# Two-layer graph network on one core: the second edge sort ends inside layer 0's batches, with eight pairs per batch weighed five to three

## The chip, the cores and the metric

One core of a Trainium2 chip runs the kernel. The metric is the device time of one execution in microseconds, and the time of the kernel before is the median of three such runs. The profile is of one more execution.

## The reference, cut to what matters

6250 nodes of 512 features, 100,000 edges (src, dst). Layer 0 is a graph attention with 8 heads of 64: for each head, the attention of an edge is a softmax over the edges of its source node, and the weighted features of the destinations are summed per source. Layer 1 sums features over the edges by destination, convolves them, and adds an attention of the first 256 nodes.

```python
feat = x @ W[h]
logit = leaky_relu(alpha_s[src] + alpha_d[dst], 0.2)
e = exp(logit - segment_max(logit, src)[src])
att = e / segment_sum(e, src)[src]
agg = segment_sum(att[:, None] * feat[dst], src)
...
agg = segment_sum(xn[edge_index[0]], edge_index[1]) / max(deg, 1)
conv_out = relu(agg @ W_conv + b_conv)
```

Layer 0 therefore needs the edges sorted by source (sort A), layer 1 the edges sorted by destination (sort B).

## The kernel before, in words

**The front.** Both sorts are bitonic over 2^17 keys, laid out as 128 rows of 1024. VectorE does a stage as two instructions, a minimum (line 2263) and a maximum (line 2264) of 128x512 each (`stage`). The merges from 2^11 to 2^17 each need the rows turned twice: a crossing is eight transposes on TensorE (line 2431, into `psA` for A, into `psCD` for B), a copy of one half by ScalarE (line 2095), and then as many stages as the merge has. Crossing n of a sort (n = 0 to 13) is followed by n/2+1 stages when n is even and by 10 when n is odd; after an odd one comes a change of sign, done by ScalarE for A and by VectorE (line 2272) for B. `ORDER` is the sequence A0 B0 A1 B1 ... A13 B13, which all three engines follow. Between crossings TensorE and ScalarE make layer 0's features, one tile of 128 nodes at a time (`dense`, `turn_h`, `project`, 49 tiles), and `DENSE_AT` says how many tiles go ahead of which crossing of A. B13, the last crossing, with its ten stages, is done on VectorE after the tables of sort A have been made (lines 2334 to 2408), and `slot_fields_of_destinations` (lines 2369 to 2374) then makes `minorB` and `sorted_nodes`.

**Layer 0.** The sorted edges are taken in 55 batches of 16 chunks of 128 edges. GpSimd gathers a batch as 16 indirect DMAs of 128 feature rows (line 517) into a ring of two batches; a slot is free when the lot (a pair of chunks, eight to a batch) that used it two batches earlier has been summed (`lot_ps`). For each batch a chain gives the weights: ScalarE copies the destinations' part of the rows when they have arrived (line 580), TensorE adds, ScalarE copies the logits (line 582), VectorE finds the maxima (`local_runs`, `carry_runs`, `find_tops`, lines 622 to 678), ScalarE takes the exponential (line 560), TensorE turns the weights (line 795). Then the pairs of chunks are weighed: pairs 0 to 5 by VectorE (line 694), 6 and 7 by ScalarE (`weigh_late`, line 568, 16 activations of 128x65 a pair); TensorE multiplies each by a one-hot matrix (`lot`, line 812), and VectorE adds the lot to its tile (`add_lot`, line 704). `OWN = LB - 2` is the number of VectorE's pairs.

What sets the order is `pass_batch(this, nxt)`, written out per engine: while lot a of this batch is done, a step of the next batch's chain is put behind it (on VectorE local_runs at a = 4, find_tops at a = 5, its first two weighings at a = 7). VectorE, ScalarE and TensorE run it as a loop over two batches.

```python
OWN = LB - 2
for a in range(OWN, LB - 1):
    weigh_late(this, a)
...
if 2 <= a + 2 < OWN:
    weigh(this, a + 2)
```

**Layer 1.** Its first steps on VectorE (`layer1_vector`) take the first node of chunks from `sorted_nodes`, then scale and normalise the tiles (line 1333, `x1_slots`), while TensorE does the attention of 256 nodes; then GpSimd gathers again (line 1141).

## Time and profile before

| | us |
|---|---|
| median of three runs (2983.2 to 2986.25) | 2983.75 |
| the profiled execution's own time | 2989.12 |
| its span | 2987.2 |
| TensorE busy in the span | 2509.0 (84%) |
| VectorE busy | 2172.7 (73%) |
| GpSimd busy | 1835.8 (61%) |
| ScalarE busy | 993.7 (33%) |

The span runs from the first to the last instruction of the profiled execution. Its stages, by the timelines: the front to about 411, layer 0's batches to about 1560, layer 1's attention and tables to about 1700, its gathers to about 2700, the convolution and the output to the end. Busy shares are means over all of them, so a stage has to be looked at by itself.

### The profile page before, as it was taken

Reading aid. Unit: us, or ns where it says so; the run is one execution under the profiler, and the core shown is the slowest. Engines: PE = TensorE matmul, PEld = TensorE weight load, DVE = VectorE, ACT = ScalarE, POOL = GpSimd, SP = SyncE. Lnnn points to the kernel's source line nnn. Section 1 sums busy time; section 2 is a strip of 40 time slices with the busy share of each in tenths; the row PEclk is TensorE's granted clock in tenths of the full one; section 3 lists DMA queues with packets and bytes.
Section 4 is the critical chain, followed back from the end, with each engine's and each line's share of the span. In section 5 each row is a group of like instructions: output and inputs, shape, how many; then the busy total and the mean of one; then the engine's idle time right before and its main releaser. Section 6 shows DMA issues by size and latency. Waiting matters only on the chain. (4 is left out here: it accounts for less than half of the span.)

```text
span 2987.2 us, 46040 instructions
## 1 busy us (share of the span) xinstructions
PE 2509.0 (84%) x10691; PEld 1549.3 (52%) x10692; DVE 2172.7 (73%) x3788; ACT 993.7 (33%) x3078; POOL 1835.8 (61%) x1881
## 2 busy tenths in 40 slices
PE   5887728999999999999988888888888889999990
PEld 4555416777777777777766733333333333334440
DVE  8999988898888888888988655434444444445668
ACT  6843335555555555555553600000000000002220
POOL 0000036777777777777748267777777777774658
PEclk8998858999999999999997999999999999999995
DMA  6110047888888888888757877777777777774217
GB/s 208 52 40 37 37 136 217 240 243 246 243 239 245 245 239 245 244 244 240 245 189 227 269 247 210 210 210 209 210 210 210 210 210 210 210 209 124 67 56 295
DMA packets 243450, 588.26 MB, mean 197 GB/s; under 512 B 57744, under 2 KB 82832, under 8 KB 243400
## 3 DMA queue, kind: packets, MB, share of 16 engines
q0 software_dynamic: 133120, 443.52, 50.6%
q1 hardware_dynamic: 110280, 144.14, 14.7%
q8 instruction: 23, 0.38, 0.0%
q14 instruction: 27, 0.22, 0.0%
HBM read 533.43 MB, written 54.10 MB: 197 GB/s over the span
## 5 line engine op out<-in xcount | busy, mean ns | idle before, releaser
L517 POOL DMA_INDIRECT big<-feat_table,idx x880 | 839.0, 953 | 688.1 <-ACT idx L542 408.1
L1141 POOL DMA_INDIRECT big<-h_table,idx x784 | 741.4, 946 | 303.3 <-issue 216.2
L812 PE MATMUL psA<-big,onehot 128*128 128x260 f32 x1760 | 440.3, 393 | 16.1 <-DVE big L694 13.9
L812 PE MATMUL psB<-big,onehot 128*128 128x260 f32 x1760 | 433.7, 390 | 7.3
L568 ACT ACTIVATE big<-big,late_weights 128x65 f32<-128x65 f32 x1760 | 434.1, 340 | 0.0
L812 PEld LDWEIGHTS psA<-big,onehot 128*128 128x128 f32 x1760 | 318.3, 191 | 100.4 <-issue 37.0
L812 PEld LDWEIGHTS psB<-big,onehot 128*128 128x128 f32 x1760 | 317.7, 190 | 63.8 <-DVE acc L704 17.6
L542 ACT CAST idx<-minorB 128x8 int32 (+1 forms) x101 | 20.2, 203 | 944.0 <-DMA big<-h_table,idx 944.0
L1570 DVE TENSOR_TENSOR acc<-acc,psCD 128x512 f32 x176 | 120.6, 685 | 205.1 <-PE psCD L1879 203.1
L1570 DVE TENSOR_TENSOR acc<-acc,psA 128x512 f32 x176 | 120.6, 685 | 202.6 <-PE psA L1879 199.9
L1878 PE MATMUL psCD<-big,onehot 128*128 x352 | 185.1, 607 | 45.4 <-ACTq L1294 39.3
L1878 PE MATMUL psA<-big,onehot 128*128 x352 | 184.8, 607 | 42.7 <-ACTq L1294 37.4
L694 DVE TENSOR_TENSOR big<-big,psCD 128x1040 f32<-128x1040 f32 x168 | 204.1, 1229 | 0.0
L694 DVE TENSOR_TENSOR big<-big,psE 128x1040 f32<-128x1040 f32 x162 | 196.8, 1228 | 0.0
L2464 PE MATMUL psB<-big 128*128 128x512 f32 x392 | 184.8, 616 | 0.0
L1905 PE MATMUL psA<-big 128*128 128x512 f32 x392 | 180.8, 605 | 0.0
L1879 PE MATMUL psCD<-big,onehot 128*128 x352 | 179.8, 593 | 0.0
L1879 PE MATMUL psA<-big,onehot 128*128 x352 | 179.8, 593 | 0.0
L704 DVE TENSOR_TENSOR acc<-acc,psA 128x520 f32 x220 | 152.8, 694 | 26.4 <-DVE acc L704 12.6
L704 DVE TENSOR_TENSOR acc<-acc,psB 128x520 f32 x220 | 152.1, 691 | 7.6 <-PE psB L812 3.3
L552 ACT CAST onehot<-psCD 128x1024 f32<-128x1024 bf16 x110 | 111.7, 1015 | 128.2 <-PE psB L812 128.2
L1570 DVE TENSOR_TENSOR acc<-acc,psE 128x512 f32 x88 | 60.3, 685 | 111.5 <-PE psE L1879 110.6
(446 smaller groups left out, 3841.8 us busy)
## 6 DMA issues: line engine op xcount, KB each, us to landing
nodes_all<-slot_nodes SPq DMA_DIRECT2D x56, 512.0 KB
big<-feat_table,idx POOLq DMA_INDIRECT x880, 3.8
feat_table<-big SPq DMA_DIRECT2D x49, 264.0 KB, 2.1
x_table<-acc SPq DMA_DIRECT2D x49, 256.0 KB, 5.8
h_table<-big SPq DMA_DIRECT2D x49, 256.0 KB, 3.7
big<-h_table,idx POOLq DMA_INDIRECT x784, 3.7
big<-h_table SPq DMA_DIRECT2D x49, 256.0 KB, 2.6
big<-x_table SPq DMA_DIRECT2D x49, 256.0 KB, 4.2
```

Source lines behind the costliest of these rows:

```text
L517: g.indirect_dma_start(ring[:, b.k, q * SB + u, :], None, feat_table, bass.IndirectOffsetOnAxis(ap=idx[:, 2 * b.k + q, u:u + 1], axis=0)). ...
L552: s.copy(onehot[:, q, :, :].rearrange("p b n -> p (b n)"), onehot_ps).then_inc(onehot_ready, 1)
L568: ins = s.activation(part, part, ACT.Copy, scale=late_weights[:, at:at + 1])
L694: v.tensor_tensor(pair, pair, weight_ps[b.k][:, 2 * a * H:(2 * a + 2) * H] .rearrange("p (b h) -> p b h", h=H).unsqueeze(3).broadcast_to([ ...
L704: v.tensor_tensor(d, d, (psA, psB)[a % 2][:, :].rearrange("p (u w) -> p u w", u=2)[:, :, 0:HALF_W], ALU.add).then_inc(lot_added, 1)
L812: ins = pet.matmul(psum[:, 512 * hf:512 * hf + HALF_W], onehot[:, q, u % SB, :], ring[:, b.k, u, HALF_W * hf:HALF_W * (hf + 1)], start=(u ...
L1141: g.indirect_dma_start(big[:, place:place + D], None, h1_table, bass.IndirectOffsetOnAxis(ap=idx[:, r.c % CHUNK_CYCLE, b:b + 1], axis=0)). ...
L1570: v.tensor_tensor(d, d, lot1_sums(r, b), ALU.add).then_inc(lot1_added, 1)
L1878: pet.matmul(lot1_sums(r, b), onehot[:, r.q, 2 * b, :], pair[:, 0:D], start=True, stop=False)
L1879: pet.matmul(lot1_sums(r, b), onehot[:, r.q, 2 * b + 1, :], pair[:, D:2 * D], start=False, stop=True).then_inc(lot1_ps, 1)
L1905: ins = pet.matmul(psA[:, q * 512:(q + 1) * 512], aggT[:, q, k * P:(k + 1) * P], Wc_s[:, k, :], start=(k == 0), stop=(k == KD - 1))
L2464: pet.matmul(psB[:, q * D:(q + 1) * D], hTbuf[:, q, k * P:(k + 1) * P], W4[:, k, :, :].rearrange("p h o -> p (h o)"), start=(k == 0), stop ...
```

## The change

Sort B's crossings 8 to 13 (the merges to 2^15, 2^16 and 2^17) leave the front. Their 48 stages (5+10+6+10+7+10) are spread over layer 0's batches by `LatePlan`: 36 batches get one stage and 6 get two (batches 2, 7, 18, 24, 35 and 42, `doubles` = 1), always behind `add_lot` of a = 3. Each of the six crossings is done in two halves in two batches of their own (four transposes on TensorE after lot 6, one copy of 128x512 on ScalarE after the feed); in 9 of those 12 batches VectorE has no stage. ScalarE does the two late changes of sign. VectorE weighs pairs 0 to 4, ScalarE 5, 6 and 7. The remaining crossings of B are cut into parts between A's (`B_PARTS`), and `DENSE_AT` has new numbers. The loops over batches on VectorE, ScalarE and TensorE are written out (SyncE and GpSimd keep theirs). `minorB` and `sorted_nodes` are made in layer 1's first steps. The late stages use `tables` and a new `late_keys`, in whose space `minorB` and `nodeB` lie; the tile table and the pads share `pad_space`.

```diff
+        FRONT_BITS = 14
+        FRONT_B = 2 * (FRONT_BITS - ROW_BITS)
+        B_PARTS = {0: [(0, 0, 17)], 1: [(1, 0, 5)], 2: [(1, 5, 17)], 3: [(2, 0, 17)], 4: [(3, 0, 5)], 5: [(3, 5, 17)], 6: [(4, 0, 17)], 7: [(5, 0, 5)], 8: [(5, 5, 17)], 9: [(6, 0, 17)], 10: [(7, 0, 4)], 11: [(7, 4, 7)], 12: [(7, 7, 17)]}
+        ORDER = [(kind, n) for na in range(CROSSINGS)
+                 for kind, n in [("A", na)] + [("B", nb) for nb, first, _ in B_PARTS.get(na, ()) if first == 0]]
+        assert [n for kind, n in ORDER if kind == "B"] == list(range(FRONT_B))
+        DENSE_AT = {("A", n): count for n, count in enumerate((17, 0, 4, 1, 4, 1, 3, 1, 3, 2, 3, 2, 3, 2))}
...
+                at, batch, turned = self.first_at, 0, FRONT_B
+                self.stages, self.crossings, self.copied, self.flips = {}, {}, {}, {}
+                for n in range(FRONT_B, CROSSINGS):
+                    m = ROW_BITS + 1 + n // 2
+                    needed = step
+                    for half in range(2):
+                        turned, step = turned + 1, step + 1
+                        self.crossings[batch + half] = (half, needed, at, turned)
+                        self.copied[batch + half] = step
+                    at, batch = at ^ 1, batch + 2
+                    js = list(range(ROW_BITS - 1, -1, -1) if n % 2 else range(m - ROW_BITS - 1, -1, -1))
+                    first = batch
+                    while js:
+                        count = 2 if batch - first < doubles else 1
+                        for j in js[:count]:
+                            self.stages.setdefault(batch, []).append((j, step, at))
+                            at, step = at ^ 1, step + 2
+                        js, batch = js[count:], batch + 1
+                    batch -= 1
+                    if n % 2 and m < ALL_BITS:
+                        self.flips[batch] = (m + 1, step, at)
+                        at, step, batch = at ^ 1, step + 1, batch + 1
+                self.last_step = step
+                assert at == 0 and batch < BATCHES, (at, batch)
...
-        OWN = LB - 2
+        OWN = LB - 3
...
-                                pool.wait_ge(sortB_done, 2)
+                                pool.wait_ge(look_ready, 1)
...
+            def late_copies(t):
+                if t in late.flips:
+                    m, step, at = late.flips[t]
+                    act.wait_ge(sortB.step, step)
+                    s.activation(late_bufs[at ^ 1], late_bufs[at], ACT.Identity,
+                                 scale=signs[:, m - ROW_BITS:m - ROW_BITS + 1]).then_inc(sortB.step, 1)
+                if t in late.crossings:
+                    half, _, at, turned = late.crossings[t]
+                    act.wait_ge(sortB.turned, turned)
+                    s.copy(late_bufs[at ^ 1][:, half * 512:(half + 1) * 512], (psD, psE[:, :])[t % 2]).then_inc(sortB.step, 1)
...
-            with act.Fori(0, BATCHES // 2) as i:
-                for c in range(2):
-                    feed(Batch(i, c + 1), Batch(i, c))
+            for n in range(BATCHES - 1):
+                feed(batch(n + 1), batch(n))
+                late_copies(n)
...
+            def late_stage(j, step, at):
+                dve.wait_ge(sortB.step, step)
+                a, b = (late_bufs[at].rearrange("p (n two h) -> p n two h", two=2, h=1 << j)[:, :, u, :] for u in range(2))
+                low, high = (late_bufs[at ^ 1].rearrange("p (n two h) -> p n two h", two=2, h=1 << j)[:, :, u, :]
+                             for u in range(2))
+                v.tensor_tensor(low, a, b, ALU.min).then_inc(sortB.step, 1)
+                v.tensor_tensor(high, a, b, ALU.max).then_inc(sortB.step, 1)
...
                             tiles = load_tiles(dve, tileA, this(2, 1))
+                            for j, step, at in late.stages.get(this.c, ()):
+                                late_stage(j, step, at)
...
-            with dve.Fori(0, BATCHES // 2) as i:
-                for c in range(2):
-                    pass_batch(Batch(i, c), Batch(i, c + 1))
+            for n in range(BATCHES - 1):
+                pass_batch(batch(n), batch(n + 1))
             pass_batch(batch(BATCHES - 1), None)
...
+                    if a == LB - 2 and this:
+                        cross_late(this.c)
+                    if a == 4 and this and this.c - 1 in late.copied:
+                        pe.wait_ge(sortB.step, late.copied[this.c - 1])
...
+            def cross_late(t):
+                if t in late.crossings:
+                    half, needed, at, _ = late.crossings[t]
+                    pe.wait_ge(sortB.step, needed)
+                    for b in range(4):
+                        block = (4 * half + b) * P
+                        ins = pet.transpose((psD, psE[:, :])[t % 2][:, b * P:(b + 1) * P], late_bufs[at][:, block:block + P], ident)
+                    ins.then_inc(sortB.turned, 1)
...
-            turn_fields(sortB, 2)
             pass_batch(None, batch(0))
-            pe.wait_ge(sortB_done, 2)
-            with pe.Fori(0, BATCHES // 2) as i:
-                for c in range(2):
-                    pass_batch(Batch(i, c), Batch(i, c + 1))
+            for n in range(BATCHES - 1):
+                pass_batch(batch(n), batch(n + 1))
...
+            act.wait_ge(fields, 2)
             PA.done(s.copy(node_rows, sorted_nodes), "nodes")
+            PA.wait(act, "nodes")
...
-            dve.wait_ge(sortB_done, 2)
+            dve.wait_ge(sortB.step, late.last_step)
+            v.tensor_scalar(sorted_nodes, late_bufs[0].bitcast(I32), SHIFT, MINOR_MASK, ALU.logical_shift_right,
+                            ALU.bitwise_and).then_inc(fields, 1)
+            dve.wait_ge(fields, 2)
...
+            x1_upto(3)
+            low, wrap = keys_flat[:, 0:COLS].bitcast(I32), late_bufs[0].bitcast(I32)
+            dve.wait_ge(fieldsT, 3)
+            link(v.tensor_scalar(low, psC[:, :].bitcast(I32), MINOR_MASK, None, ALU.bitwise_and))
+            link(v.tensor_scalar(wrap, low, float(PAD_MINOR), -float(PAD_MINOR), ALU.is_ge, ALU.mult))
+            v.tensor_tensor(minorB[:, :, :].rearrange("p b r -> p (b r)"), low, wrap, ALU.add).then_inc(sortB_done, 1)
...
+            pe.wait_ge(sortB.step, late.last_step)
+            pe.wait_ge(parts_kept, BATCHES + 1)
+            for b in range(SB):
+                ins = pet.transpose(psC[:, b * P:(b + 1) * P], late_bufs[0][:, b * P:(b + 1) * P], ident)
+            ins.then_inc(fieldsT, 1)
...
+            pe.wait_ge(sortB_done, 1)
...
+                for i, j in list(enumerate(js))[first:end]:
+                    stage(srt, j, False, srt.ps if i == 0 else srt.bufs[:, srt.at, :], srt.bufs[:, srt.at ^ 1, :], True)
+                if n % 2 and m < ALL_BITS and end >= len(js):
+                    if srt is sortB and n == FRONT_B - 1:
+                        dve.wait_ge(srt.step, srt.steps)
+                        v.tensor_scalar(late_bufs[late.first_at], srt.bufs[:, srt.at, :],
+                                        signs[:, m + 1 - ROW_BITS:m + 2 - ROW_BITS], None, ALU.mult).then_inc(srt.step, 1)
+                        srt.steps += 1
+                    else:
+                        flip(srt, m + 1)
```

And in the program of the front:

```diff
-            for kind, n in ORDER[:-1]:
-                if (kind, n) == ("A", 1):
+            for na in range(CROSSINGS):
+                if na == 1:
                     group_rstd0(2)
-                sort_crossed({"A": sortA, "B": sortB}[kind], n)
+                sort_crossed(sortA, na)
+                for nb, first, end in B_PARTS.get(na, ()):
+                    sort_crossed(sortB, nb, first, end)
...
-            sort_crossed(sortB, CROSSINGS - 1)
-            kB, other = sorted_keys_of(sortB)
             dve.wait_ge(rows_loaded, 16)
             for q in range(2):
                 v.tensor_scalar(onehotT[q], nodes_all[:, q, :], iota_col[:, 0:1], None, ALU.is_equal).then_inc(onehotT_ready, 1)
-            slot_fields_of_destinations(kB, other, minorB)
```

How the order moves, at three places. VectorE, the middle of a batch (around `add_lot` of a = 2 and 3; 694/743 is a weighing, 704/753 an `add_lot`, 632/681 the first step of local_runs). Before:

```order
L703 REGISTER_ALU
L704 ISA
L704 TENSOR_TENSOR acc<-acc,psA 128x520
L694 TENSOR_TENSOR big<-big,psCD 128x2x520
L700 REGISTER_ALU
L703 REGISTER_ALU
L704 ISA
L704 TENSOR_TENSOR acc<-acc,psB 128x520
L131 ISA
L131 TENSOR_LOAD tables
L631 REGISTER_ALU
L632 SCALAR_TENSOR_TENSOR alphas<-alphas 128x128
```

Now, in a batch with one stage:

```order
L743 TENSOR_TENSOR big<-big,psE 128x2x520
L753 ISA
L753 TENSOR_TENSOR acc<-acc,psA 128x520
L753 ISA
L753 TENSOR_TENSOR acc<-acc,psB 128x520
L135 TENSOR_LOAD pad_space
L761 TENSOR_TENSOR tables<-late_keys 128x128x4
L762 TENSOR_TENSOR tables<-late_keys 128x128x4
L681 SCALAR_TENSOR_TENSOR alphas<-alphas 128x128
```

The weighing that stood between the two `add_lot` is gone, and a minimum and a maximum between `tables` and `late_keys` stand ahead of local_runs.

ScalarE, from the one-hot copy that ends one feed to the next batch's copy of the destinations' part (580/620). Before:

```order
L552 CAST onehot<-psCD 128x1024
L568 ACTIVATE big<-big,late_weights 128x65 x16
L577 REGISTER_ALU
L580 COPY look_space<-big 128x128
L581 REGISTER_ALU
L582 COPY alphas<-psCD 128x128
L551 REGISTER_ALU
L552 CAST onehot<-psCD 128x1024
```

Now, in a batch that holds half a crossing:

```order
L592 CAST onehot<-psCD 128x1024
L643 COPY late_keys<-psCD 128x512
L608 ACTIVATE big<-big,late_weights 128x65 x32
L620 COPY look_space<-big 128x128
L622 COPY alphas<-psCD 128x128
L592 CAST onehot<-psCD 128x1024
L582 CAST idx<-minorA 128x8 x2
L608 ACTIVATE big<-big,late_weights 128x65 x16
```

32 activations instead of 16 stand ahead of that copy, and in twelve batches the copy of half a crossing as well.

TensorE in the front, from crossing A2 on (2431/2515 is a crossing, `psA` for A and `psCD` for B; 2452, 2464 and 2469 or 2536, 2548 and 2553 are one tile). Before:

```order
L2431 MATMUL psA<-ident_wide,big 128x128 x8
L2431 MATMUL psCD<-ident_wide,big 128x128 x8
L2431 MATMUL psA<-ident_wide,big 128x128 x8
L2431 MATMUL psCD<-ident_wide,big 128x128 x8
L2452 MATMUL psCD<-ident_wide,big 128x128 x4
L2464 MATMUL psB<-big 128x512 x4
L2469 MATMUL psE<-Wa,big 128x16 x4
```

Now:

```order
L2515 MATMUL psA<-ident_wide,big 128x128 x8
L2536 MATMUL psCD<-ident_wide,big 128x128 x4
L2548 MATMUL psB<-big 128x512 x4
L2553 MATMUL psE<-Wa,big 128x16 x4
L2515 MATMUL psA<-ident_wide,big 128x128 x8
L2515 MATMUL psCD<-ident_wide,big 128x128 x8
L2536 MATMUL psCD<-ident_wide,big 128x128 x4
L2548 MATMUL psB<-big 128x512 x4
L2553 MATMUL psE<-Wa,big 128x16 x4
```

A tile stands between A2 and A3, and B2 has moved behind A3, with the next four tiles (the first is shown) behind it.

## Rows read from the trace of the kernel before

**Rows 1.** Work by engine in stretches: busy (instructions) per engine, granted clock, DMA share, GB/s
```profile
150.00:225.00 75.00, 66.07 (x300) 43.18 (x300) 70.77 (x113) 30.40 (x67) 0.00 (x0) 0.93 0.11 40
225.00:300.00 75.00, 60.46 (x264) 38.66 (x264) 73.26 (x116) 26.94 (x60) 0.00 (x0) 0.86 0.10 37
900.00:1100.00 200.00, 182.18 (x1078) 141.97 (x1076) 178.24 (x360) 112.10 (x410) 151.45 (x160) 1.00 0.82 244
```

**Rows 2.** Timeline of GpSimd: start, duration, engine, line, operation, [idle before <- releaser]
```profile
411.44 1.13 POOL L517 DMA_INDIRECT big<-feat_table,idx  x1 [407.49 <-ACT idx L542]
...
466.24 0.94 POOL L517 DMA_INDIRECT big<-feat_table,idx  x1 [4.55 <-PE psA L812]
...
1530.04 0.94 POOL L517 DMA_INDIRECT big<-feat_table,idx  x1 [0.30 <-issue]
...
1700.77 1.05 POOL L1141 DMA_INDIRECT big<-h_table,idx  x1 [49.98 <-DMA h_table<-big]
```

**Rows 3.** Timeline of VectorE in the sort
```profile
157.40 0.69 DVE L2263 TENSOR_TENSOR big<-big,psA 128x512 f32<-128x512 f32 x1
...
223.03 0.69 DVE L2263 TENSOR_TENSOR big<-big 128x512 f32<-128x512 f32 x1
...
224.36 0.69 DVE L2263 TENSOR_TENSOR big<-big 128x512 f32<-128x512 f32 x1
...
252.02 0.75 DVE L2272 TENSOR_SCALAR big<-big,signs 128x1024 f32<-128x1024 f32 x1
...
404.75 0.69 DVE L2334 TENSOR_SCALAR big<-big 128x1024 int32<-128x1024 int32 x1
```

**Rows 4.** Timeline of TensorE in the same stretch
```profile
240.76 0.64 PE L2452 MATMUL psCD<-ident_wide,big 128*128 128x128 f32 x4
...
245.47 1.07 PE L2431 MATMUL psA<-ident_wide,big 128*128 128x128 f32 x8
252.83 1.97 PE L2431 MATMUL psCD<-ident_wide,big 128*128 128x128 f32 x8 [6.28 <-DVE big L2272]
...
261.15 1.07 PE L2431 MATMUL psA<-ident_wide,big 128*128 128x128 f32 x8
```

**Rows 5.** Timeline of VectorE between the sort and the first batch
```profile
445.65 0.49 DVE L2416 TENSOR_SCALAR onehotT<-nodes_all,iota_col 128x1024 bf16<-128x1024 bf16 x1 [8.75 <-DMA nodes_all<-slot_nodes]
...
446.45 0.69 DVE L2369 TENSOR_SCALAR big<-big 128x1024 int32<-128x1024 int32 x1
...
453.52 0.28 DVE L632 SCALAR_TENSOR_TENSOR alphas<-alphas 128x128 f32<-128x128 f32 x1
```

**Rows 6.** Groups of instructions of GpSimd in 417.7:424.2, 425.2:436.3 and 1000:1400
```profile
L517 POOL DMA_INDIRECT big<-feat_table,idx x6 | 5.7, 946 | 1.8 <-issue 1.8
...
L517 POOL DMA_INDIRECT big<-feat_table,idx x9 | 9.3, 1033 | 2.7 <-issue 2.7
...
L517 POOL DMA_INDIRECT big<-feat_table,idx x320 | 304.2, 951 | 97.5 <-issue 87.7 <-PE psB L812 4.9 <-PE psA L812 4.9
```

**Rows 7.** Timeline of ScalarE in one batch
```profile
1003.67 3.95 ACT L568 ACTIVATE big<-big,late_weights 128x65 f32<-128x65 f32 x16
1011.74 0.30 ACT L580 COPY look_space<-big 128x128 f32<-128x128 f32 x1 [4.13 <-DMA big<-feat_table,idx]
...
1022.45 1.01 ACT L552 CAST onehot<-psCD 128x1024 f32<-128x1024 bf16 x1 [2.33 <-PE psB L812]
```

**Rows 8.** Timeline of VectorE in the same batch
```profile
1001.52 2.38 DVE L694 TENSOR_TENSOR big<-big,psE 128x1040 f32<-128x1040 f32 x2
...
1012.92 0.33 DVE L632 SCALAR_TENSOR_TENSOR alphas<-alphas 128x128 f32<-128x128 f32 x1
...
1021.28 2.38 DVE L694 TENSOR_TENSOR big<-big,psCD 128x1040 f32<-128x1040 f32 x2
```

**Rows 9.** Timeline of TensorE, lot 5 of that batch and layer 1's first transposes
```profile
1014.92 1.97 PE L812 MATMUL psB<-big,onehot 128*128 128x260 f32 x8
...
1576.08 1.97 PE L1740 MATMUL psCD<-ident_wide,look_space 128*128 128x128 f32 x8 [8.07 <-ACT look_space L1184]
```

83 lines of the change are left out of this document (37 added, 46 removed).

## The prediction

> **What bounds the kernel now.** I first read the work by engine in stretches, since a share over the span mixes stages. In the front VectorE is busy 94 to 98% [rows 1], TensorE 81 to 88%: the sorts on VectorE set the pace, with TensorE close behind, and TensorE's granted clock falls from 0.93 to 0.86 where it waits more. In layer 0's batches every engine looks full. What bounds them is on GpSimd's timeline: the first gather goes out at 411.44, the first one that had to wait for a lot at 466.24, the last of the 880 at 1530.04 [rows 2]. From 466.24 on that is 847 steps in 1063.8 us, 1.256 us each, and the group of 320 gathers in 1000:1400 has 0.951 busy and 0.30 between two, mostly "issue" [rows 6]: GpSimd never stops. A batch is 16 gathers, 20.1 us. The other engines wait for rows: ScalarE stood idle 4.13 us for a DMA ahead of line 580 [rows 7]. So a microsecond saved on VectorE inside a batch is worth nothing, and one that is added costs nothing while the loop stays under 20.1.
>
> How near is it? VectorE's own loop, from one late_weights copy's first weighing to the next, is 1001.52 to 1021.28, 19.76 us, with hardly a gap ahead of 1012.92 [rows 8]: some 19.65 if it never waited for rows, 0.45 under GpSimd. And there is a cushion: batch 2's first gather is the one at 466.24, so the gather that reuses lot 5's slot of batch 27 (442 steps later) goes out at 1021.4, while that lot ends at 1016.9 [rows 2, 9]. The engines can be 4.5 us late before GpSimd stops.
>
> **The front.** A stage costs 224.36 - 223.03 = 1.33 us, a change of sign 0.75 [rows 3]. Crossings B8 to B12 have 5+10+6+10+7 = 38 stages ahead of sort A's tables, which begin at 404.75: 50.5 us, and two changes of sign, 1.5: 52.0 us off VectorE's path. B13's ten stages (another 13 us) give nothing: they ran while VectorE would otherwise have waited for the nodes, and it still waited 8.75 us after them [rows 5].
>
> Not all of the 52 comes. TensorE's tiles stay (4.71 us each, 240.76 to 245.47), and after an idle of 6.28 us a crossing and a tile took 8.32 us where 1.07 + 4.71 = 5.78 is normal, 2.5 more [rows 4]; this goes with the lower granted clock of that stretch [rows 1]. In the new order TensorE waits at B2 until B1's last five stages are done, and only then has B2 and four tiles ahead of A4: 1.07 + 18.8 + 2.5 + 1.07 + 0.8 for ScalarE's copy (an estimate: half the elements of the 1.01 us copy in rows 7, and two waits) = 24.3 us, while VectorE has A3's ten stages and B2's two, 15.9. Stall: 8.4 us. The same count gives 21.8 - 19.9 = 1.9 at A2 (four tiles behind B1, against 15 stages), about 1.0 at A7 and 2.7 at A10 (three tiles and ScalarE's change of sign against 14 stages); at the others VectorE has more to do than TensorE. Sum 14.0, so the tables start **38.0 us earlier**. Bounds for the stalls: 0 (the front now has next to none, rows 1) and 28, twice my count, because a late tile moves all that follow.
>
> **Up to the first lot.** The nodes' DMA chain hangs on the tables of sort A and moves with them. Behind it `slot_fields_of_destinations` goes away, from 446.45 to 453.52, 7.07 us [rows 5]. Part of it covered the look-up, copies and logits of batch 0, which TensorE and ScalarE did beside it and which VectorE must now wait for. Between 0 and 7.1 I take the middle, **3.4 us**. GpSimd then starts batch 2 some 41.4 us earlier than 466.24, though it waits some 11 us in front of it: 32 gathers at 1.256 take 40 us, and the lot it needs comes 51 us after the first gather.
>
> **Layer 0.** VectorE per batch: one weighing less, 2.38 - 1.23 = 1.15 us [rows 8], and in 36 batches one stage more, 1.33 and about 0.1 for its wait: 19.93, under 20.1. In six batches there are two stages, 21.3, and each makes the loop 1.2 us late, which the cushion of 4.5 takes, and the 13 batches without a stage (18.5) give it back. ScalarE per batch: a pair more, 3.95 us, ahead of line 580, where it stood idle 4.13 [rows 7]: it now arrives 0.2 us before the rows. From 1011.74 to its next one-hot copy at 1022.45 is 10.7, and copy and two pairs are 8.8 more: 19.5. In twelve batches a copy of half a crossing and in two a change of sign come on top, each at most about the 1.01 us of that one-hot copy [rows 7]: 20.5, again within the cushion. Lot 5 now waits for ScalarE: its pair is done about 3.95 us behind 1003.67, so at 1007.6, and the lot starts at 1014.92 [rows 7, 9]. TensorE's 48 late transposes are a half-dozen crossings, 1.07 each. The written-out loops I cost at nothing; they issue one program row after another as the front does, and the cover is the same cushion.
>
> So GpSimd stays the bound, and what counts is what slows a gather. In 425.2:436.3, while VectorE ran B13's stages, nine gathers had a mean of 1.033 us; in 417.7:424.2, six had 0.946 [rows 6]. That is 0.087 us per gather of 1.33 us, so per stage, and 48 stages make **4.2 us**. By the Trainium skill, page "SBUF — State Buffer", section "SBUF: two separate sides", VectorE and GpSimd share a pair of ports as an exclusive lock, which an operation with two SBUF inputs also takes against a GpSimd operation that reads SBUF, and the loser blocks for the whole instruction. The stages have two SBUF inputs, the weighings one; by that rule 96 instructions could each hold a gather for up to their 0.69 us, 66 us in all. The trace shows a sixteenth of it.
>
> **Layer 1.** Inserted ahead of its first tiles are the field of the nodes (0.69 us, as line 2369) and, behind tile 2, three operations of the same kind as lines 2372 to 2374; TensorE's first transposes, at 1576.08 [rows 9], wait for these. VectorE's part is between 0, were it all beside waits, and the 7.07 us that the same four operations and their turn took in a row [rows 5]; the turn is now done before VectorE comes to it, which leaves less than half, and the first transposes follow VectorE closely, so I take **3.0 us**, and it stays to the end because the gathers from 1700.77 [rows 2] are again GpSimd's.
>
> **Sum:** -38.0 - 3.4 + 4.2 + 3.0 = -34.2 us. Against the profiled execution's 2989.12 that is 2954.9; the median of the runs is 5.4 lower, so 2983.75 - 34.2 = **2949.5 us**.
>
> **The rivals.**
> 1. TensorE takes over the front. For it: it is busy 81 to 88% there already [rows 1], and the clock falls with every wait. Against: at most crossings VectorE's stages outlast the tiles. If the stalls are 28 instead of 14, the time is 2963.5.
> 2. VectorE's loop becomes layer 0's bound. For it: only 0.2 us lie between 19.93 and 20.1, and each stage stands straight ahead of the chain that makes the weights. Against: the loop now has gaps of its own that the counts keep. If the weighing's 1.15 us don't come back, because VectorE only waits for lots instead, a batch with a stage takes 21.08: 0.9 times 36, and 2.2 times 6, less the cushion of 4.5, is 41 us, and the time 2983.75 - 34.2 + 41 - 4.2 (GpSimd's slowing no longer counts) = 2986. A third of it (0.3 us a batch) gives about 2959.
> 3. The lock is held. For it: the same two engines, and gathers of 1.033 against 0.946 us [rows 6]. Against: the size. If each late stage stops GpSimd for its 1.38 us, 48 of them are 66 us, the sum -34.2 - 4.2 + 66 = +27.6 and the time 3011. It decides against the change from (34.2 + 4.2) / 48 = 0.8 us a stage on. The Trainium skill's page "SBUF — State Buffer" is the rule behind this one.
> 4. The change doesn't do what it says: the tables of sort A wait for something else, such as the last tile's features or ScalarE's clearing of `acc` behind them. These hang on the last tile, which is ahead of A13's ten stages; then perhaps 10 us of 38 are lost, 2960.
>
> **How the numbers follow.** Forecast 0.70 (with rival 1's milder forms in it); rival 1 in full 0.09; rival 2 in its mild form 0.07 and in full 0.05; rival 3 0.04; rival 4 0.05. The forecast's own ends are the stalls at 0 with no slowing of gathers (2949.5 - 14 - 4.2 = 2931) and rival 1 in full (2963.5). To hold 8 in 10 the range goes on over rival 4 and the mild form of 2, and a little beyond for both at once: 2931 to 2973. What a measurement can tell from no change is about 0.2%, 6 us. Faster by more: 0.90; within it (rival 2 in full): 0.04; slower by more: 0.06.
>
> **What would show it.** First gather of layer 0 at about 373 instead of 411.44; VectorE stopping for some 8 us ahead of A4; the first waiting gather at about 425. Then 847 steps in about 1068 us with 0.951 to 0.96 busy a gather, and "issue" as what ends nearly all its gaps. ScalarE's wait for the DMA ahead of its copy falls from 4.13 to almost nothing. I am wrong if GpSimd's gaps in layer 0 end with TensorE's lots (rival 2), if gathers show durations of 1.5 us and more (rival 3), or if TensorE has no idle left in the front (rival 1).

## The result, and the profile after

The changed kernel takes **2962.43 us** (median of 4 runs, 2959.41 to 2966.27) against 2985.0 for the kernel before (4 runs, 2983.2 to 2991.3): a ratio of 0.9922, 95% interval 0.991 to 0.9934. It is 22.6 us faster; forecast were 34.2. Five more runs, beside nine of the kernel before, gave 0.9926 (0.9913 to 0.994). The time lies in the forecast's range, with two thirds of the gain.

The profiled execution took 2959.41 us with a span of 2957.6, 29.6 less than the span before. GpSimd's timeline, as [rows 2] (start, duration, line, and the idle time with what ended it):

```profile
371.65 1.13 POOL L557 DMA_INDIRECT big<-feat_table,idx  x1 [367.70 <-ACT idx L582]
...
422.13 0.95 POOL L557 DMA_INDIRECT big<-feat_table,idx  x1 [9.17 <-PE psA L870]
...
1496.27 0.94 POOL L557 DMA_INDIRECT big<-feat_table,idx  x1 [0.30 <-issue]
...
1670.57 1.05 POOL L1210 DMA_INDIRECT big<-h_table,idx  x1 [51.65 <-issue]
```

These four times cut the run into the terms of the forecast:

| stretch | before | after | difference | forecast |
|---|---|---|---|---|
| up to the first gather | 411.44 | 371.65 | -39.8 | -38.0 |
| from there to the first gather that waits for a lot | 54.80 | 50.48 | -4.3 | -3.4 |
| its 847 steps, layer 0 | 1063.80 | 1074.14 | +10.3 | +4.2 |
| last gather to layer 1's first | 170.73 | 174.30 | +3.6 | +3.0 |
| from there to the end of the span | 1286.43 | 1287.03 | +0.6 | 0 |

The work by engine in the stretches of [rows 1] (the first row's VectorE fell from 70.77 to 62.77 us by its waits; in the last row ScalarE rose from 112 to 151 by the third pair, and GpSimd is as full as it was):

```profile
150.00:225.00 75.00, 66.17 (x301) 43.46 (x302) 62.77 (x100) 30.98 (x68) 0.00 (x0) 0.91 0.11 40
225.00:300.00 75.00, 59.77 (x254) 38.22 (x253) 73.06 (x115) 25.63 (x57) 0.00 (x0) 0.86 0.10 36
900.00:1100.00 200.00, 181.36 (x1055) 141.14 (x1055) 174.92 (x362) 150.70 (x569) 151.99 (x158) 0.99 0.82 242
```

**The front.** VectorE's waits for ScalarE's copies of TensorE's crossings, and what TensorE did ahead of the second one shown:

```profile
179.35 0.69 DVE L2350 TENSOR_TENSOR big<-big,psA 128x512 f32<-128x512 f32 x1 [1.88 <-ACT big L2182]
...
212.38 0.69 DVE L2350 TENSOR_TENSOR big<-big,psA 128x512 f32<-128x512 f32 x1 [7.42 <-ACT big L2182]
...
307.85 0.69 DVE L2350 TENSOR_TENSOR big<-big,psA 128x512 f32<-128x512 f32 x1 [3.45 <-ACT big L2182]
```
```profile
189.32 1.97 PE L2515 MATMUL psCD<-ident_wide,big 128*128 128x128 f32 x8 [5.13 <-DVE big L2359]
...
210.55 1.07 PE L2515 MATMUL psA<-ident_wide,big 128*128 128x128 f32 x8
```

The forecast's stalls were 1.9 at A2, 8.4 at A4, 1.0 at A7 and 2.7 at A10; they are 1.88, 7.42, 0.23 and 3.45. The 21.2 us between the two TensorE rows are B2's crossing and four tiles. TensorE had stood idle 5.13 us ahead of them, while VectorE had work; then VectorE waited 7.42 us for the fourth tile.

**Layer 0.** GpSimd's groups in 1000:1400, before in [rows 6], and after:

```profile
L557 POOL DMA_INDIRECT big<-feat_table,idx x316 | 304.9, 965 | 96.3 <-issue 84.4 <-PE psA L870 6.4 <-PE psB L870 5.5
```

The gaps are still 0.30 us and mostly "issue", so GpSimd sets the pace as before. What has grown is the gather itself, 0.965 us where it was 0.951. Where, the timelines of GpSimd and of VectorE in one batch tell (707.53 is the last lot's add ahead of the late stage, 708.14 its min, 708.75 its max):

```profile
706.08 0.95 POOL L557 DMA_INDIRECT big<-feat_table,idx  x1 [0.30 <-issue]
707.33 0.94 POOL L557 DMA_INDIRECT big<-feat_table,idx  x1 [0.30 <-issue]
708.58 1.07 POOL L557 DMA_INDIRECT big<-feat_table,idx  x1 [0.31 <-issue]
```
```profile
706.64 0.69 DVE L753 TENSOR_TENSOR acc<-acc,psA 128x520 f32 x1
707.53 0.69 DVE L753 TENSOR_TENSOR acc<-acc,psB 128x520 f32 x1 [0.20 <-DVE acc L753]
708.14 0.69 DVE L761 TENSOR_TENSOR tables<-late_keys 128x512 f32<-128x512 f32 x1
708.75 0.68 DVE L762 TENSOR_TENSOR tables<-late_keys 128x512 f32<-128x512 f32 x1
```

The gather at 707.33 ran through an add from PSUM and the start of the min and took 0.94. The one at 708.58 began while the min ran, until 708.83, and took 1.07. In another batch the max reached further into the gather:

```profile
1012.92 1.32 POOL L557 DMA_INDIRECT big<-feat_table,idx  x1 [0.30 <-issue]
```
```profile
1012.74 0.68 DVE L762 TENSOR_TENSOR late_keys<-tables 128x512 f32<-128x512 f32 x1
```

Here the max ends 0.50 us after the gather's start, and the gather is 0.37 longer. In the first case the min ends 0.25 after it, and the gather is 0.12 longer. Both suggest one rule, **theory M**: a VectorE operation with both inputs in SBUF that is under way when a gather begins holds it from about 0.12 us after its start until the operation ends.

**ScalarE** still waited a little for the rows ahead of its copy of the logits, 4.13 in [rows 7]:

```profile
992.57 0.30 ACT L620 COPY look_space<-big 128x128 f32<-128x128 f32 x1 [0.79 <-DMA big<-feat_table,idx]
...
1013.46 0.30 ACT L620 COPY look_space<-big 128x128 f32<-128x128 f32 x1 [1.58 <-DMA big<-feat_table,idx]
```

**Between the sort and the first lot.** VectorE's waits for the nodes, where [rows 5] has one of 8.75:

```profile
402.76 0.49 DVE L2501 TENSOR_SCALAR onehotT<-nodes_all,iota_col 128x1024 bf16<-128x1024 bf16 x1 [19.74 <-DMA nodes_all<-slot_nodes]
...
409.13 0.49 DVE L665 TENSOR_SCALAR onehotT<-nodes_all,iota_col 128x1024 bf16<-128x1024 bf16 x1 [5.22 <-DMA nodes_all<-slot_nodes]
```

The second wait is new. The next batch's load of the nodes lands some 6 us behind the first, and before, `slot_fields_of_destinations` filled that time. (There the second of the two operations began 7.47 us behind the first, at 453.12; here it is 6.37 us behind, and between 6.1 and 7.7 in the other six profiles below that have this front.)

**Layer 1's preamble.** VectorE's rows of the inserted work, and TensorE's first transposes, as [rows 9]:

```profile
1530.78 0.68 DVE L1481 TENSOR_SCALAR onehot<-tables 128x1024 int32<-128x1024 int32 x1
...
1531.49 0.89 DVE L1484 COPY small<-onehot 128x4 int32<-128x4 int32 x1
1532.41 0.97 DVE L1485 TENSOR_SCALAR small<-small 128x4 int32<-128x4 int32 x1
1533.41 0.97 DVE L1486 CAST small<-small 128x4 f32<-128x4 int32 x1
...
1543.76 1.21 DVE L1496 TENSOR_SCALAR big<-psCD 128x1024 int32<-128x1024 int32 x1
1545.00 1.36 DVE L1497 TENSOR_SCALAR tables<-big 128x1024 int32<-128x1024 int32 x1
1546.40 1.95 DVE L1498 TENSOR_TENSOR late_keys<-big,tables 128x1024 int16<-128x1024 int32 x1
```
```profile
1548.40 1.97 PE L1827 MATMUL psCD<-ident_wide,look_space 128*128 128x128 f32 x8 [11.04 <-DVE late_keys L1498]
```

The field pushes three operations on four numbers into the time in which GpSimd's scaling of `acc` (line 573, from 1531.18) runs. They take 0.9 us each, and each ends 0.03 us behind the end of one of GpSimd's operations (1532.35, 1533.35, 1534.35); in the kernel before the same three took 0.15 to 0.17, the last of them begun at 1564.92, just ahead of that scaling at 1564.93:

```profile
1564.53 0.15 DVE L1409 CAST small<-nodeB 128x4 int32<-128x4 int16 x1
...
1564.92 0.17 DVE L1411 CAST small<-small 128x4 f32<-128x4 int32 x1
```

### The profile page after: what moved, and what is told of

It reads as the page before. It is cut to its first block and busy times, and to the rows that moved or that the text cites. A ratio compares the mean times of both kernels' runs of the same rounds, so it can differ in the third digit from the quotient of the medians.

```text
span 2957.6 us, 44079 instructions
## 1 busy us (share of the span) xinstructions
PE 2492.7 (84%) x10647; PEld 1541.3 (52%) x10692; DVE 2091.6 (71%) x3730; ACT 1208.4 (41%) x3966; POOL 1846.5 (62%) x1881
## 5 line engine op out<-in xcount | busy, mean ns | idle before, releaser
L557 POOL DMA_INDIRECT big<-feat_table,idx x880 | 848.8, 965 | 644.4 <-ACT idx L582 367.7
L608 ACT ACTIVATE big<-big,late_weights 128x65 f32<-128x65 f32 x2640 | 645.0, 340 | 0.0
L582 ACT CAST idx<-late_keys 128x8 int32 (+1 forms) x101 | 20.2, 203 | 944.5 <-DMA big<-h_table,idx 944.5
L870 PEld LDWEIGHTS psB<-big,onehot 128*128 128x128 f32 x1760 | 317.2, 190 | 58.3 <-issue 11.9
L743 DVE TENSOR_TENSOR big<-big,psCD 128x1040 f32<-128x1040 f32 x140 | 169.5, 1227 | 0.0
L743 DVE TENSOR_TENSOR big<-big,psE 128x1040 f32<-128x1040 f32 x135 | 163.5, 1228 | 0.0
```

The costliest lines, as they stand in the source:

```text
L557: g.indirect_dma_start(ring[:, b.k, q * SB + u, :], None, feat_table, bass.IndirectOffsetOnAxis(ap=idx[:, 2 * b.k + q, u:u + 1], axis=0)). ...
L608: ins = s.activation(part, part, ACT.Copy, scale=late_weights[:, at:at + 1])
L743: v.tensor_tensor(pair, pair, weight_ps[b.k][:, 2 * a * H:(2 * a + 2) * H] .rearrange("p (b h) -> p b h", h=H).unsqueeze(3).broadcast_to([ ...
L870: ins = pet.matmul(psum[:, 512 * hf:512 * hf + HALF_W], onehot[:, q, u % SB, :], ring[:, b.k, u, HALF_W * hf:HALF_W * (hf + 1)], start=(u ...
```

## The experiments

Two theories stood against M for layer 0's loss: C, each stage costs the same wherever it stands, and L, the loss comes from the written-out loops or from ScalarE's third pair. The table has, from each profile, the first gather, the time from the first gather that waits for a lot to the last, the time from there to layer 1's first, the span, and the ratio of the times.

| kernel | first gather | layer 0 | to layer 1 | span | ratio (95%) |
|---|---|---|---|---|---|
| before | 411.44 | 1063.80 | 170.73 | 2987.2 | 1 |
| after | 371.65 | 1074.14 | 174.30 | 2957.6 | 0.9922 (0.991 to 0.9934) |
| after_again | 372.54 | 1074.74 | 174.69 | 2968.6 | 0.9926 (0.9913 to 0.994) |
| apart | 371.30 | 1074.58 | 174.24 | 2962.9 | 0.9938 (0.9924 to 0.9952) |
| early | 372.92 | 1086.04 | 173.70 | 2973.0 | 0.9965 (0.9951 to 0.9979) |
| own2 | 372.08 | 1090.95 | 173.21 | 2974.6 | 0.998 (0.9967 to 0.9993) |
| before_own3 | 411.35 | 1062.86 | 170.68 | 2985.6 | 0.9994 (0.9985 to 1.0004) |
| before_unrolled | 412.25 | 1066.48 | 167.34 | 2982.2 | 1.001 (0.9997 to 1.0022) |
| front_b2 | 367.70 | 1072.57 | 173.15 | 2951.6 | 0.9907 (0.9891 to 0.9922) |
| front_more | 364.47 | 1074.73 | 173.06 | 2953.9 | 0.9897 (0.9884 to 0.9911) |
| turn_psA | 374.85 | 1072.73 | 174.01 | 2960.3 | 0.9935 (0.9915 to 0.9955) |
| layer1_later | 371.25 | 1072.98 | 171.92 | 2952.1 | 0.991 (0.9897 to 0.9924) |
| both | 365.40 | 1073.81 | 171.66 | 2946.2 | 0.9872 (0.9854 to 0.9889) |

**The kernel itself again (after_again).**

> The changed kernel itself once more, as the measure for its variants in the same set. Both theories: median between 2959 and 2967 us, 0.990 to 0.9935 of the kernel before; first gather near 371.6 us, last gather near 1496.3 us, mean gather in layer 0 0.963 us.

Median 2963.05 us, and the same stretches, except that this execution's last part took 1293.1 us instead of 1287.0 and the start of layer 0 53.5 instead of 50.5. So single spans of one kernel differ by 11 us, while the stretches up to the first gather, in layer 0 and up to layer 1 repeat within 1 us. Over all kernels below that have the same instructions in a stretch the scatter is wider: the first gather lies at 371.25 to 374.85 in seven, layer 0 at 1072.57 to 1074.74 in seven, the way to layer 1 at 173.06 to 174.69 in seven (of own2's, only the last batch's weighing differs). The verdicts below rest on these stretches, and a difference under 2 us in one of them (under 4 for the first gather) is not told from scatter.

**The same stage one lot earlier (early).**

```diff
                         add_lot(this, a, tiles[a % LOTS])
+                        if stages and a + 2 == LOTS:
+                            late_stage(*stages[0])
                         if a + 1 == LOTS:
                             tiles = load_tiles(dve, tileA, this(2, 1))
-                            for j, step, at in late.stages.get(this.c, ()):
-                                late_stage(j, step, at)
+                            for stage in stages[1:]:
+                                late_stage(*stage)
```

> Only the place changes: a batch's first late stage, min and max in a row, goes from behind the fourth lot's add to behind the third's. Theory M (moment): by the distances in the changed kernel's trace the min then starts 0.0 to 0.1 us after a gather's start and covers its moment, so one gather a stage is held 0.4 to 0.5 us (gathers of 1.35 to 1.46 us) instead of 0.12: 42 x 0.35 = some 15 us slower than the changed kernel, less if the engines settle at another distance. Theory C (count): 0 within 1.5 us, as many operations as before. Theory L: 0.

Layer 0 took 1086.04 us, 11.9 more than the changed kernel, with the very same instructions; the median is 2974.78 against 2963.05. C and L said 0, so neither can be the whole cause. Its GpSimd timeline has such gathers in nearly every batch with a stage, beside VectorE's min and max:

```profile
857.52 0.95 POOL L557 DMA_INDIRECT big<-feat_table,idx  x1 [0.30 <-issue]
858.77 1.42 POOL L557 DMA_INDIRECT big<-feat_table,idx  x1 [0.30 <-issue]
```
```profile
858.69 0.69 DVE L761 TENSOR_TENSOR tables<-late_keys 128x512 f32<-128x512 f32 x1
859.29 0.69 DVE L762 TENSOR_TENSOR tables<-late_keys 128x512 f32<-128x512 f32 x1
```

The min begins 0.08 us before the gather and ends 0.61 after its start; 0.61 less 0.12 is 0.49, and the gather is 0.47 longer. The max, begun behind that gather's start, adds nothing.

**Min and max with an add between them (apart).**

```diff
+                    if stages and a + 2 == LOTS:
+                        late_half(0, *stages[0])
                     if this:
                         add_lot(this, a, tiles[a % LOTS])
+                        if stages and a + 2 == LOTS:
+                            late_half(1, *stages[0])
...
```

`late_half(0, ...)` is the min of a stage and `late_half(1, ...)` its max, both on one line now, 761; the second stage of the six double batches stays behind the fourth lot's add.

> Only the place of a batch's first late stage changes: its min goes ahead of the third lot's add and its max behind it, so that an operation on PSUM stands between the two. Theory M (moment): a gather touches SBUF about 0.12 us after its start, and is held only by a VectorE operation with two SBUF inputs that covers that moment, until this operation ends. In the changed kernel's trace the min ends 0.24 us behind the gather's start, so each single stage holds one gather by 0.12 us. Placed apart, by the distances in that trace, the min would end before one gather's moment and the max before the next one's: the gathers of 1.05 to 1.08 us beside single stages go, 42 x 0.12 = 5 us come back in layer 0, the time is about 5 us below the changed kernel's (the six double stages keep theirs). Theory C (count): each stage costs what it costs wherever it stands, so 0 within 1.5 us. Theory L (loops: the slowing comes from the written-out loops or ScalarE's third pair): 0.

No gain: 1074.58 in layer 0 where 5 us less were expected. The forecast of distances failed, not the rule. In 23 of the 42 batches with a stage no gather was held by it; in the other 19 a min, or a second stage's max, came 0.03 to 0.26 us ahead of a gather and held it 0.3 us and more, like this pair of rows (GpSimd, VectorE):

```profile
832.82 1.25 POOL L557 DMA_INDIRECT big<-feat_table,idx  x1 [0.30 <-issue]
```
```profile
832.57 0.68 DVE L761 TENSOR_TENSOR late_keys<-tables 128x512 f32<-128x512 f32 x1
```

The distance between the engines depends on what was held before, so one place meets gathers in two different ways. Going through the timelines of this kernel, 23 late operations were under way at a gather's start and ended over 0.1 us behind it, and for all 23 the gather's duration is 0.95 plus that end less 0.12, within 0.02 us. The sums of what the late operations added are 6.4 us in the changed kernel (41 gathers), 8.4 here (23) and 16.6 in the early one (42): 0.13, 0.17 and 0.35 us for each of 48 stages.

**ScalarE back to two pairs (own2).**

```diff
-        OWN = LB - 3
+        OWN = LB - 2
```

> The changed kernel with ScalarE weighing two pairs of a batch as before, and VectorE six: the late stages stay. Forecast's step (a weighing of 1.15 us less on VectorE makes room for the stage): VectorE's loop is 21.1 us in 36 batches, 22.4 in six and 19.65 in 13, against GpSimd's 20.3, so GpSimd's gaps of 0.30 us grow where it waits for lots: (0.8 x 36 + 2.1 x 6 - 0.65 x 13, less the cushion of 4.5) = 28 us slower than the changed kernel. Rival (VectorE has room of its own between waits, and ScalarE's third pair buys nothing): 0 to 3 us.

Layer 0 took 1090.95 us, 16.8 more than with three pairs, and GpSimd now waits for lots:

```profile
581.85 0.94 POOL L557 DMA_INDIRECT big<-feat_table,idx  x1 [1.57 <-PE psB L870]
...
644.95 0.94 POOL L557 DMA_INDIRECT big<-feat_table,idx  x1 [1.67 <-PE psB L870]
...
650.49 0.95 POOL L557 DMA_INDIRECT big<-feat_table,idx  x1 [0.85 <-PE psB L870]
```

Of the 16.8 us, 13.7 are longer gaps ahead of gathers (271.8 us in sum against 258.1) and the rest longer gathers. That is less than 28, so VectorE's loop has some slack that the count didn't know (where, no run shows), but the weighing does make the room for the stages.

**Each side change alone, in the kernel before (before_own3, before_unrolled).** The first is the line above, with `late_weights` 6 * H wide; the second:

```diff
-            with dve.Fori(0, BATCHES // 2) as i:
-                for c in range(2):
-                    pass_batch(Batch(i, c), Batch(i, c + 1))
+            for n in range(BATCHES - 1):
+                pass_batch(batch(n), batch(n + 1))
```

and likewise on ScalarE and TensorE.

> The kernel before with only the weighing moved: ScalarE three pairs, VectorE five; no late stages, loops as they were. GpSimd bounds layer 0, so 0 within 2 us in time; ScalarE's wait ahead of its copy of the rows falls from 4.13 to about 0.2 us. Theory L (the slowing of gathers comes from ScalarE's third pair or another phase of the loops): mean gather from 0.951 to 0.955 to 0.96 us and 3 to 6 us slower.

> The kernel before with only the loops over batches of ScalarE, VectorE and TensorE written out, as the change has them. Forecast: 0 within 2 us, the first rows issued as the front issues them. Theory L: the fetching of more program takes DMA time from the gathers' rows or moves the engines: mean gather or gap longer, 3 to 6 us slower. A gain is possible too if the loops' registers and branches cost something on the path, up to 2 us.

The third pair alone leaves layer 0 where it was (1062.86), and ScalarE's wait falls from 4.13 to 0.74 us (by the mean of some 50 batches, from 4.34 to 0.59). The written-out loops alone cost it 2.7 us, with a mean gather of 0.954 instead of 0.951, and both times are level with the kernel before. GpSimd's groups between the first waiting gather and the last (480:1530, and 440:1490 for the changed kernel) of before, before_own3, before_unrolled and the changed kernel:

```profile
L517 POOL DMA_INDIRECT big<-feat_table,idx x837 | 796.0, 951 | 255.0 <-issue 227.2 <-PE psA L812 14.6 <-PE psB L812 12.5
```
```profile
L517 POOL DMA_INDIRECT big<-feat_table,idx x835 | 793.4, 950 | 254.3 <-issue 225.7 <-PE psA L812 16.1 <-PE psB L812 12.5
```
```profile
L517 POOL DMA_INDIRECT big<-feat_table,idx x835 | 796.8, 954 | 254.3 <-issue 223.3 <-PE psA L810 15.5 <-PE psB L810 14.9
```
```profile
L557 POOL DMA_INDIRECT big<-feat_table,idx x828 | 797.8, 963 | 252.3 <-issue 223.1 <-PE psA L870 15.2 <-PE psB L870 14.0
```

So of the 10.3 us, 6.4 are the stages. Of the other 3.9, by the durations of the gathers, 2.9 are VectorE's one-hot operations (line 616, 615 and 665 in the three kernels), which were there before: they lengthen 33 gathers by 3.6 us in sum, where they lengthened 11 by 0.7. The scans of the running maxima hold gathers too, but changed little (2.7 us in sum before, 2.9 after). The one-hot operations have one tile in SBUF as input, not two, and they hold a gather in two places. Under way at its start, they act as theory M says (224 of 253 cases). But theory M leaves the second place out, which the kernel before_unrolled shows best (GpSimd, VectorE):

```profile
773.41 1.08 POOL L517 DMA_INDIRECT big<-feat_table,idx  x1 [0.30 <-issue]
```
```profile
773.29 0.68 DVE L703 TENSOR_TENSOR acc<-acc,psA 128x520 f32 x1
773.90 0.47 DVE L615 TENSOR_SCALAR big<-nodes_all,iota_col 128x1024 bf16<-128x1024 bf16 x1
```

The add at 773.29 has an input in PSUM; an add in that place holds no gather elsewhere. The one-hot operation begins 0.49 us behind the gather's start, and the gather ends 0.12 us behind its end. Over the thirteen profiles 125 one-hot operations began 0.40 to 0.50 us behind the start of a gather that no other operation held: 104 kept the gather until 0.12 or 0.13 us behind their own end, up to 1.09 us, and in the other 21 the operation itself took some 0.72 us instead of 0.47 and the gather its 0.95. 31 late min or max began 0.36 to 0.50 us behind such a start and lengthened none. Of the 2.7 us of the written-out loops 2.5 are of this second kind (26 such gathers against 5). That the loops do it by the distance of the engines is argued from this, not shown by a run of its own.

**One tile ahead of B2's crossing (front_b2), and the tiles spread further (front_more).**

```diff
+        DENSE_AT[("A", 4)], DENSE_AT[("B", 2)] = 3, 1
```
```diff
+        for crossing, tiles_ahead in ((("B", 2), 1), (("A", 4), 2), (("A", 6), 4), (("B", 6), 1), (("A", 10), 2)):
+            DENSE_AT[crossing] = tiles_ahead
```

> One of the four tiles ahead of sort A's fifth crossing is projected ahead of sort B's third crossing instead, where TensorE stood idle 5.13 us. Theory T (TensorE's wait ahead of that crossing is what VectorE's 7.42 us wait is made of): the wait of VectorE falls from 7.4 to about 2.7 us, the first gather goes from 371.65 to about 367 us, and all that follows comes as much earlier: 4 to 5 us below the changed kernel. Rival: ScalarE's copies or the lower granted clock set that wait, and it moves to the next crossing: less than 1 us.

> The changed kernel with TensorE's tiles spread otherwise over the crossings of the front: one ahead of sort B's third and one ahead of its seventh crossing, where TensorE stood idle 5.13 and 3.37 us, sort A's fifth has two instead of four, its seventh four instead of three, its eleventh two instead of three. Theory T (each of VectorE's waits is the tile that TensorE still had to do while it had been idle before): VectorE's waits of 7.42 and 3.45 us go, and no new one over 1 us appears: first gather at 362 to 363 us instead of 371.6 to 372.5, some 9 us less than the changed kernel in all. Rival (as front_b2 left 3.50 us of the wait: the tiles' copies on ScalarE lag too): first gather at 365 to 367 us.

VectorE's wait at A4 became 3.50 us and the first gather came 4 us earlier; spread further, both large waits fell to 1.4 us:

```profile
208.27 0.69 DVE L2351 TENSOR_TENSOR big<-big,psA 128x512 f32<-128x512 f32 x1 [3.50 <-ACT big L2183]
```
```profile
206.23 0.69 DVE L2352 TENSOR_TENSOR big<-big,psA 128x512 f32<-128x512 f32 x1 [1.43 <-ACT big L2184]
...
313.34 0.69 DVE L2352 TENSOR_TENSOR big<-big,psA 128x512 f32<-128x512 f32 x1 [1.36 <-ACT big L2184]
```

The first gather is at 364.47, between the theory's 362 to 363 and the rival's 365 to 367. What front_b2 left of the wait is ScalarE's: TensorE did the crossing only after the change of sign on line 2190, and ScalarE did that behind the last tile's copies.

```profile
206.42 1.09 PE L2516 MATMUL psA<-ident_wide,big 128*128 128x128 f32 x8 [2.12 <-ACT big L2190]
```

In front_more the change of sign starts as soon as VectorE is done, at 202.31; the change (1.15 us), the crossing (1.97) and ScalarE's copy (0.58) are then more than the two stages of B that VectorE has beside them (2.7), and the 1.43 us are what is left. The median of front_b2 fell by 7 us (2956.01 against 2963.05), which is more than its first gather explains.

**Layer 1: only the turn moved (turn_psA), then the work itself (layer1_later).** The first turns the late keys into `psA`, so that the first transposes need not wait for VectorE:

```diff
...
-                ins = pet.transpose(psC[:, b * P:(b + 1) * P], late_bufs[0][:, b * P:(b + 1) * P], ident)
+                ins = pet.transpose(psA[:, b * P:(b + 1) * P], late_bufs[0][:, b * P:(b + 1) * P], ident)
...
-            pe.wait_ge(sortB_done, 1)
             pe.wait_ge(hA_ready, NT)
...
             SACT.wait(pe, "hT")
+            pe.wait_ge(sortB_done, 1)
```

The second, in short:

```diff
+            link(v.tensor_scalar(first_tile_i, late_bufs[0].bitcast(I32)[:, 0:COLS:2 * P], SHIFT + 7, MINOR_MASK >> 7,
+                                 ALU.logical_shift_right, ALU.bitwise_and))
+            link(v.tensor_copy(first_tile, first_tile_i))
             dve.wait_ge(lot_added, ADD_CREDIT + ROWS * LOTS)
...
             x1_upto(17)
+            low, wrap = keys_flat[:, 0:COLS].bitcast(I32), late_keys[:, COLS // 2:COLS].bitcast(I16)
```

with the three operations on `low` and `wrap` behind it, the field of the nodes behind tile 13, and ScalarE's copy of the turned keys to `low` ahead of its first deviations.

> The changed kernel with the late keys turned into the PSUM tile of the lots instead of the one that layer 1's first transposes use; only the product behind the transposes waits for the three inserted operations. Forecast's step (the inserted operations are on the path because the first transposes wait for them, 3.0 us, 3.6 in the trace): the transposes start 2 us earlier, and the first gather of layer 1 comes 1 to 3 us earlier. Rival (VectorE's time itself, 4.5 us for the three, is what is late, not the wait): less than 0.5 us.

> The changed kernel with the work that it inserted ahead of layer 1's first tiles put elsewhere: the four numbers per partition that the first product needs are taken straight from the keys ahead of the reciprocal (two short operations), the field of all nodes comes behind tile 13, ScalarE copies the turned keys out of PSUM, and the three operations on them come behind tile 17. Theory V (VectorE's own time ahead of the first groups of tiles is what is late: some 3 us for the field and for three short operations of 0.9 us beside GpSimd's, 4.5 us for the three): TensorE's first transposes come 46 us behind the last gather instead of 52.1, and layer 1's first gather 170.7 us behind it or less, instead of 174.0: 3 to 4 us less. Rival (as the kernel that only moved the turn showed, something behind takes it back): less than 1 us.

TensorE's rows, of turn_psA and of layer1_later:

```profile
1548.21 1.97 PE L1826 MATMUL psCD<-ident_wide,look_space 128*128 128x128 f32 x8 [8.07 <-ACT look_space L1253]
...
1581.38 3.57 PE L1856 MATMUL psCD<-half,onehot 128*128 128x2 f32 x16 [6.80 <-ACT look_space L1310]
```
```profile
1542.89 1.94 PE L1829 MATMUL psCD<-ident_wide,look_space 128*128 128x128 f32 x8 [9.19 <-ACT look_space L1257]
```

With only the turn moved the transposes came 48.8 us behind the last gather instead of 52.1, but TensorE then waited 6.80 us for ScalarE (4.55 in the changed kernel), whose squares stand behind deviations that hang on VectorE's tiles: 0.3 us was left at layer 1's first gather, which is nothing against the scatter, and the median (2962.92) is level with the changed kernel. With the work moved behind the early tiles the transposes came at 46.2, the gather at 171.92, 2.4 us better (1.1 us under the lowest of the seven with the changed kernel's work there), and the median was 2955.36, 28 below the kernel before beside it. Theory V holds in direction and for the transposes; at layer 1's first gather it gave less than its 3 to 4. The part behind that gather was some 3.5 us shorter too (1283.5, and 1282.7 in the last kernel). By the profiles this lies behind layer 1's last gather, in 289.4 and 290.1 us from there to the end instead of 293.8, where the edit changes no instruction; no run separates that.

**Both.**

The edits of front_more and of layer1_later in one kernel.

> Both edits together: the gains add, since one lies ahead of the first gather and the other behind the last: 12 us less than the changed kernel, 2950 us, 0.9885 of the kernel before. If they don't add, GpSimd's gathers would have to be held more in between (mean over 0.967 us instead of 0.965).

**2945.7 us**, 0.9872 of the kernel before (0.9854 to 0.9889): 17 us less than the changed kernel, where 12 were expected. Its first gather is at 365.40 and layer 1's 171.66 behind the last, 6 to 7 and 2 to 3 us better, as in the two kernels alone; the surplus is in the part behind, 1282.7. The mean of all 880 gathers is 0.964, level with the changed kernel's 0.963.

## Why the prediction was right, and where not

- **What bounds each part** was right: the front by VectorE, layer 0 by GpSimd's gathers before and after, and what is saved ahead of the first gather reaches the end.
- **The front, -38.0:** -39.8. The count of tiles against stages gave each stall within 1 us, 13.0 in sum against 14.0. Rival 1 (stalls of 28) did not happen. front_b2 shows one cause of the largest stall, 3.9 of its 7.4 us: a tile that stood behind a late crossing and not ahead of it. The other part is the change of sign that ScalarE does behind the last tile's copies.
- **Up to the first lot, -3.4:** the step "I take the middle, 3.4 us" failed. The pair of profiles shows -4.3, but that one pair is luck: over all profiles this stretch is 52.5 us on average in the seven with the changed kernel's front (50.5 to 53.6) and 53.1 in the three of before's kind (52.0 to 54.8): -0.6. The second load of the nodes, not an engine, follows the first, and VectorE waits 5.22 us for it here and 5.60 in the kernel run again.
- **Layer 0, +4.2:** the step that failed is the size, "0.087 us per gather of 1.33 us, so per stage". Measured are 0.13 for a stage, 6.4 us for 48, and 3.9 us for what stood there before, one-hot operations at new distances above all, a term that the forecast put at nothing. The error was to take the mean of nine gathers as a property of the stage. It is one of the distance between two engines; the same stage costs 0.35 one lot earlier.
- **Rival 3, the lock:** by the Trainium skill's page "SBUF — State Buffer", section "SBUF: two separate sides", an operation with two SBUF inputs takes the shared ports as a lock. The trace agrees: the adds and weighings, with one input in PSUM, account for none of the lengthened gathers, the min and max with two in SBUF do, and the gather goes on when they end. The price that I took from the rule, a whole operation of 0.69 us for each of 96, does not come about: only 41 of them were under way at a gather's start, each held it for what was left of it, 0.16 us on average, and one that began behind a gather's start did not lengthen it and took its usual 0.68 to 0.72 us, where by the rule the gather, which started first, would have kept the ports. At 0.8 us a stage the change would have lost; it was six times less.
- **Rival 2, VectorE's loop:** no. own2 shows how near it is: without the third pair 16.8 us are lost in layer 0.
- **Layer 1, +3.0:** +3.6, right in size, in part by luck. The three short operations, cost at nothing, made up with the field half of the delay of the transposes (52.1 against 46.0 us behind the last gather), and of these 6.1 us later waits took 2.5 back.
- **The sum:** the profiles give -29.6, the medians -22.6. With averages in place of single profiles (first gather at 372.4 in those seven, 411.7 in those three) the first four stretches are -39.3 - 0.6 + 10.3 + 3.6 = -26.0. The last 3 to 4 us are not shown. Some 2 may lie in what follows layer 1's first gather: with the changed kernel's instructions it took 1286.0 to 1293.1 us, 1288.3 on average in six profiles, and 1284.1 to 1288.2, 1286.3 on average, in the three of before's kind. In the kernel run again, 6.1 us slower there, 2.6 lie ahead of layer 1's 33rd gather and 3.2 behind its last; what sets them apart stays open.

## What to carry to other kernels

When an operation is moved beside an engine that bounds a stage, price it by where it meets that engine's instructions, not by a mean over a stretch: the two timelines side by side give the moment and the reach, and one and the same stage cost 6.4 or 16.6 us in this kernel. Work moved off a critical path is soon followed by what it had been covering; look for the next load behind it. And when two engines alternate, an idle time of one just ahead of a wait of the other is a piece of work in the wrong order, which here was worth 7 us at the first gather.

## What the hardware showed that was not expected

- A gather on GpSimd (0.95 us) is held by VectorE in two places. From about 0.12 us after its start it waits for a min, max or one-hot operation that was under way when it began, up to 0.5 us; a min or max that begins behind its start adds nothing. A bfloat16 one-hot operation that begins 0.40 to 0.50 us behind the start holds it until 0.12 us behind its own end, in 104 of 125 cases.
- The hold works the other way too: beside GpSimd's `tensor_tensor`, VectorE's three operations on four numbers took 0.89 to 0.97 us instead of 0.15 to 0.17. Not every short one is held: others beside it, as the one on line 1417 at 1540.76, took 0.15.
- Loops written out instead of run with registers, with the same work, cost layer 0 2.7 us, and the time from the last gather to layer 1's first was 3.4 us shorter (167.34 against 170.73). The time was level. Both are differences of single profiles. Why the second is so was not followed up.
